# A fused layer of top-2 experts and gated delta-rule attention: expert rows gathered raw, weighed and scattered in token order, and added by accumulating transfers

## What is computed

```
xn  = (x - mean) / sqrt(var + 1e-5)
out = x + attention(xn) + ffn(xn)

ffn:       probs = softmax(xn @ Wg)          # 8 experts
           top-2 per token, their probabilities divided by their sum
           y_e = relu(xn @ W1[e] + b1[e]) @ W2[e] + b2[e]
           out = sum over the two experts of weight * y_e
attention: q, k, v = silu(conv4(xn @ Wq)), ...   # 8 heads, DK 128, DV 64
           gated delta rule over the 2048 tokens of a sequence
           (S = S * exp(g_t); u = (v_t - k_t S) * beta_t; S += k_t u; o_t = q_t S)
           out = (rmsnorm(o) * silu(xn @ Wg)) @ Wo
```

## Time and profile before

| | |
|---|---|
| median of 3 runs | 2579.6 us (2576.35 to 2581.1) |
| profiled execution, its own time | 2567.1 us |
| its span | 2565.4 us |
| PE busy | 2163.6 us (84%) |
| DVE busy | 1899.4 us (74%) |
| ACT busy | 1296.4 us (51%) |
| POOL busy | 1117.2 us (44%) |
| moved by DMA | 135.08 MB |
| routing, experts, attention | 0 to 253, 253 to 791, 791 to 2565 us |

### The profile page before, as it was taken

How to read it: one execution, slowest core, us unless ns; L and a number is a source line. 1 busy time by engine, 2 the same in 40 slices (tenths; PEclk the granted TensorE clock), 3 DMA queues, 4 the chain that set the end, 5 groups by cost and what they waited for, 6 DMA issues and landing times.

```text
span 2565.4 us, 89934 instructions
## 1 busy us (share of the span) xinstructions
PE 2163.6 (84%) x34781; PEld 1546.6 (60%) x34782; DVE 1899.4 (74%) x3928; ACT 1296.4 (51%) x3667; POOL 1117.2 (44%) x1123
## 2 busy tenths in 40 slices
PE   4441999999996798988989889898898988889886
PEld 4331889999883455555655646556565555655555
DVE  5544442232224998999989899999989999999896
ACT  0000344444333656656566565666656666566663
POOL 3555444444442262443724436254362533526333
PEclk9999999999998899999999999999999999999998
DMA  6564222222230100101010010100101001010000
GB/s 206 195 207 131 69 69 72 72 73 73 70 104 19 36 24 25 32 17 45 20 29 23 26 41 13 39 23 26 42 8 44 23 26 36 13 45 23 25 23 23
DMA packets 106769, 135.08 MB, mean 53 GB/s; under 512 B 39584, under 2 KB 80064, under 8 KB 106176
## 3 DMA queue, kind: packets, MB, share of 16 engines
q0 software_dynamic: 23296, 60.85, 7.6%
q1 hardware_dynamic: 65952, 48.91, 6.9%
q10 hardware_dynamic: 17184, 20.49, 2.3%
HBM read 76.18 MB, written 54.00 MB: 51 GB/s over the span
## 4 chain that ended last, share of the span: by engine, by line
PE 28%; DVE 26%; issue 8%; ACT 6%; DMA 1%; SPq 1%; DVEq 0%; ACTq 0%; PEldq 0%
PE att_psA L1078 9%; DVE att_cv L1540 8%; PE att_psC L1078 6%; DVE att_lane_t L1624 3%; DVE att_lanes L1626 3%; DVE att_S L1654 2%; PE att_psS L1092 2%; PE att_psC L1160 2%; PE att_psC L1183 2%; PE att_psS L1202 2%; PE att_psA L1120 2%; DVE att_O L1662 1%; DVE att_lanes L1612 1%; ACT att_t L1421 1%; ACT att_W L1434 1%
## 5 line engine op out<-in xcount | busy, mean ns | idle before, releaser
L1540 DVE SCALAR_TENSOR_TENSOR att_cv<-att_psA,att_cw,att_cv 128x508 f32<-128x508 f32 (+2 forms) x660 | 478.7, 736 | 7.6
L1078 PE MATMUL att_psA<-att_xt,att_wqkv 128*128 128x512 f32 x880 | 439.7, 633 | 14.2 <-DMA att_xt<-xn_cols 12.7
L1874 POOL TENSOR_TENSOR att_Sd<-att_S,att_mst 128x1024 f32<-128x1024 f32 x128 | 242.9, 1903 | 464.4 <-DVE att_S L1654 441.2
L804 PE MATMUL moe_psHT<-moe_xT,moe_w1s 128*128 128x128 f32 x2176 | 268.2, 277 | 0.3 <-issue 0.3
L1078 PEld LDWEIGHTS att_psA<-att_xt,att_wqkv 128*128 128x128 f32 x880 | 158.8, 196 | 179.1 <-issue 163.8
L814 PE MATMUL moe_psY<-moe_w,moe_hT 128*128 x1088 | 257.2, 379 | 0.0
L804 PEld LDWEIGHTS moe_psHT<-moe_xT,moe_w1s 128*128 128x128 f32 x2176 | 256.6, 194 | 0.9 <-issue 0.7
L669 ACT ACTIVATE moe_hT<-moe_psHT,moe_b1T 128x128 f32<-128x128 f32 x544 | 155.2, 368 | 201.0 <-PE moe_psHT L804 199.7
L768 DVE TENSOR_TENSOR moe_y<-moe_psY,moe_b2b 128x256 f32<-128x256 f32 x136 | 57.7, 424 | 255.0 <-PE moe_psY L814 154.5
L1540 DVE SCALAR_TENSOR_TENSOR att_cv<-att_psC,att_cw,att_cv 128x508 f32<-128x508 f32 (+2 forms) x300 | 213.9, 733 | 0.6
L814 PEld LDWEIGHTS moe_psY<-moe_w,moe_hT 128*128 128x128 f32 x1088 | 196.4, 190 | 21.1
(11 more groups left out here) (238 smaller groups left out, 4390.5 us busy)
## 6 DMA issues: line engine op xcount, KB each, us to landing
expert_out<-moe_y POOLq DMA_DIRECT2D x136, 128.0 KB
route_x_in<-in_L_attn_x_dram SPq DMA_DIRECT2D x64, 128.0 KB
moe_w<-in_L_ffn_W_dram SPq DMA_DIRECT2D x16, 512.0 KB
xn_rows<-route_xn ACTq DMA_DIRECT2D x16, 512.0 KB
xn_cols<-route_xnT ACTq DMA_DIRECT2D x16, 512.0 KB
att_xt<-xn_cols SPq DMA_DIRECT2D x16, 512.0 KB, 4.2
att_xr<-in_L_attn_x_dram SPq DMA_DIRECT2D x64, 128.0 KB, 2.8
out_dram<-att_xr SPq DMA_DIRECT2D x256, 32.0 KB
```

The lines of the kernel that those rows point to most:

```text
L804: last = nc.tensor.matmul(psHT[par][:, c * P:(c + 1) * P], w1s[:, par, d, c * P:(c + 1) * P], xT[:, par, d], start=(d == 0), stop=(d == DC ...
L1078: last = MM(pair_bank(m, j)[:, h, :], wqkv[:, c, (2 * j + h) * P:(2 * j + h + 1) * P], xt[:, c, :].rearrange("p (a l t) -> p l a t", a=GRO ...
L1540: last = V.scalar_tensor_tensor(out=late, in0=by_lane(pair_bank(m, j)[:, h, :])[:, :, 0:LT - d], scalar=cw[:, 2 * j + h, TAPS - 1 - d:TAPS ...
L1874: G.tensor_tensor(new, old, bc(mst[:, par, c, 4:4 + LANES, hs], 3, DV), op=ALU.mult).then_inc(s["sd_done" if two else "sd_half"], 1)
```

## The change

Each scattered row now carries a record of 8 words: SOURCE (the token), TARGET (its row in expert_rows), WEIGHT, MEAN and RSTD; 512 bytes are still written per row. xn_rows and its stores are gone. xnT has four buffers (COLS), and its copies wait for a store only from the fifth group on. The routing loops are written out for DVE, ACT and PE. DVE fills the record: mean and reciprocal deviation per group (L307, L321), the weights per iteration (L395 to L399), for which ACT does an Exp per iteration (L491). The tables slot and wtop, and the operations after the loop that made them, are gone; two spare regions with blank records are added.

```diff
+        COLS = 4
-        xnT = sb("xnT", [P, 2, DC, GT])
+        xnT = sb("xnT", [P, COLS, DC, GT])
...
+            pool.memset(record[:, :, :], 0.0).then_inc(cleared, 1)
...
+            for l in range(LANES):
+                r = slice(CT * l, CT * l + CT)
+                pool.wait_ge(consts, made + 1 + 2 * l)
+                pool.iota(fields[r, :, :, :, SOURCE], ...).then_inc(consts, 1)
+                pool.iota(fields[r, :, :, :, TARGET], ...).then_inc(consts, 1)
...
             dve.wait_ge(tr_done, g + 3)
-            dve.wait_ge(cols_stored[par], 16 * i + 16)
-            nc.vector.tensor_copy(xnT[:, par, 1], psT[:, par, 1]).then_inc(xnT_done, 1)
+            if g >= COLS:
+                dve.wait_ge(cols_stored[g % COLS], 16 * (g // COLS))
+            nc.vector.tensor_copy(xnT[:, g % COLS, 1], psT[:, par, 1]).then_inc(xnT_done, 1)
...
+            dve.wait_ge(second_done, i + 1)
+            V.tensor_scalar(total[:, :], second[:, :], 1.0, None, ALU.add).then_inc(weighed, 1)
+            dve.wait_ge(weighed, RECIPE * i + 1)
+            V.reciprocal(records[:, i, :, 0, WEIGHT], total[:, :]).then_inc(weighed, 1)
+            dve.wait_ge(weighed, RECIPE * i + 2)
+            V.tensor_tensor(records[:, i, :, 1, WEIGHT], records[:, i, :, 0, WEIGHT], second[:, :], op=ALU.mult).then_inc(noted, 1)
+            dve.wait_ge(noted, 5 * i + 5)
             V.tensor_copy(where[:, these, :], spot[:, these, :]).then_inc(located, 1)
...
-            with dve.Fori(2, NI) as i:
+            for i in range(2, NI):
...
-                act.dma_start(xn_v[g] ..., xn[:, par]).then_inc(rows_stored[par], 16)
...
+            def second_weight(i):
+                act.wait_ge(choose, CHOOSE * i + CHOOSE)
+                act.wait_ge(noted, 5 * i)
+                nc.scalar.activation(second[:, :], gap[:, :], ACT.Exp).then_inc(second_done, 1)
```

In the expert stage POOL gathers rows of x itself; DVE normalises them and keeps target and weight (L781, L783); after the second product it copies the target (L804), adds b2 (L805) and scales by the weight (L807), and POOL scatters the tile's rows into expert_rows, where the row of token n with its k-th expert is k * 8192 + n:

```diff
+            def normalise(q, par):
+                t = 2 * q + par
+                dve.wait_ge(x_loaded[par], 16 * q + 16)
+                dve.wait_ge(xtr, t + 1)
+                shift = ids.bitcast(F32)
+                nc.vector.tensor_scalar(xs[:, par], xt[:, par], shift[:, par, MEAN:MEAN + 1], shift[:, par, RSTD:RSTD + 1],
+                                        ALU.subtract, ALU.mult).then_inc(normed, 1)
+                nc.vector.tensor_copy(facts_of(t), ids[:, par, TARGET:WEIGHT + 1]).then_inc(normed, 1)
...
-                nc.vector.tensor_tensor(y[:, par], psY[par][:, 0:D], b2b[...], op=ALU.add).then_inc(y_done, 1)
+                dve.wait_ge(normed, 2 * t + 2)
+                nc.vector.tensor_copy(target[:, par, :], facts_of(t)).then_inc(y_step, 1)
+                nc.vector.tensor_tensor(y[:, par], psY[par][:, 0:D], b2b[...], op=ALU.add).then_inc(y_step, 1)
+                dve.wait_ge(y_step, 2 * t + 2)
+                nc.vector.tensor_scalar(y[:, par], y[:, par], target.bitcast(F32)[:, par, 1:2], None, ALU.mult).then_inc(y_done, 1)
...
-                pool.dma_start(yg_v[bass.ds(t, 1)]..., y[:, par]).then_inc(y_stored[par], 16)
+                pool.indirect_dma_start(yk_d[:, :], bass.IndirectOffsetOnAxis(ap=target[:, par, 0:1], axis=0), y[:, par], None).then_inc(y_stored[par], 16)
```

In the attention the gather and the two DVE operations per chunk are gone. POOL issues four accumulating DMAs at the end of chunk 1 and four at the end of chunk 2, which add the expert rows to xr while they land:

```diff
+            def add_rows(m, k):
+                if k == 0:
+                    G.wait_ge(xr_loaded, DONE * (m + 1))
+                else:
+                    G.wait_ge(y_added[0], DONE * (m + 1))
+                for l in range(LANES):
+                    G.dma_start(xr[lane_rows(l), :, :], y_v[k, l, bass.ds(m, 1)]..., accum_op=ALU.add).then_inc(y_added[k], 16)
...
             def out(m, c):
-                wait(dve, "acc2_done", n + 1)
+                if c in (0, 2):
+                    dve.wait_ge(y_added[1], DONE * (m + 1))
```

More of the change, by code:

```diff
@@ L162, in norm_and_route @@
         region = sb("region", [P, E]); region_i = sb("region_i", [P, E], I32)
[L163 to L166, removed]
+        record = sb("record", [P, NI, RECORDS + WIDE])
+        gap = sb("gap", [P, TI]); second = sb("second", [P, TI]); total = sb("total", [P, TI])
+        e8 = [sb(f"per_expert{i}", [P, E]) for i in range(4)]
         e8i = sb("per_expert_int", [P, E], I32)
@@ L217, in _ @@
                 sp.dma_start(tile[tuple(slice(None) for _ in tile.shape)], source).then_inc(loaded, 16)
+            sp.wait_ge(consts, NCONST)
+            for k in range(2):
+                row = E * (N + P) + k * P
+                sp.dma_start(ids_d[row:row + P, 0:RECORD], blank[:, E + k, :]).then_inc(rest_stored, 16)
             sp.wait_ge(rest_known, 1)
@@ L417, in link @@
                 dve.wait_ge(step, n[0])
-            weight, total, second, gap = r1
-            tot, tiles_f, end, base, zer8, tmp8 = e8
+            tot, tiles_f, end, zer8 = e8
             V.tensor_copy(rest[0:1, :], counted[0:1, :, 0]).then_inc(rest_known, 1)
-            link(V.tensor_tensor(gap[:, :], top2[:, :], top1[:, :], op=ALU.subtract))
-            gap_at = n[0]
             link(V.tensor_tensor(tot[:, :], taken, region[:, :], op=ALU.subtract))
@@ new lines, in second_weight @@
+            def second_weight(i):
+                act.wait_ge(choose, CHOOSE * i + CHOOSE)
+                act.wait_ge(noted, 5 * i)
+                nc.scalar.activation(second[:, :], gap[:, :], ACT.Exp).then_inc(second_done, 1)
+            deviation(0, 0)
+            columns(0, 0)
+            columns(1, 1)
+            for i in range(1, NI):
+                if i == 1:
+                    second_weight(0)
+                columns(2 * i, 0)
+                if i > 1:
+                    second_weight(i - 1)
+                columns(2 * i + 1, 1)
@@ L483, in _ @@
+            second_weight(NI - 1)
             for tile, source in attention_sources:
                 act.dma_start(tile, source).then_inc(attention_loaded, 16)
[L485 to L486 removed]
             nc.scalar.activation(expa[:, :], alog[:, :], ACT.Exp).then_inc(stats["expa_done"], 1)
[L488 to L491 removed]
+            for done in cols_stored:
+                act.wait_ge(done, 16 * (NG // COLS))
@@ L530, in _ @@
             columns_logits(1, 1)
-            with pe.Fori(2, NI) as i:
+            for i in range(2, NI):
                 columns_logits(i, 0)
@@ L596, in steps @@
                         between(sum(tile) + tile[0])
-            with eng.Fori(PEEL, MT // 2 - 1) as i:
+            with eng.Fori(PEEL, MT // 2 - 2) as i:
                 for tile in ((i, 1), (i + 1, 0)):
                     step(tile, after(*tile), before(*tile))
+            for tile in ((MT // 2 - 2, 1), (MT // 2 - 1, 0)):
+                step(tile, after(*tile), before(*tile))
             last = (MT // 2 - 1, 1)
@@ L834, with attention @@
 CREDIT = 4
-def attention(nc, keep, dims, loaded_params, NPARAM, xf, xnT_d, yg_d, stat_d, of):
+def attention(nc, keep, dims, loaded_params, NPARAM, xf, xnT_d, yk_d, stat_d, of):
     B, T, N, NT, NG, MT = dims
```

188 lines of the change are left out of this document (77 added, 111 removed).

## The result

The changed kernel takes 2612.1 us (median of 4, 2610.1 to 2614.1) against 2578.3 us on the same chip: 1.0136 times the time, interval 1.0121 to 1.0152, 34 us slower (the ratios here are of the runs beside each other; the two medians alone give 1.0131). The forecast was 2605, within 2541 to 2640, and slower; the direction and the range held, the sum of 26 us was 8 too small, and its parts were further off than the sum.

The account below looks back on a forecast made before the run. Experts bound by PE, attention mostly by a PE and DVE chain, routing by DVE's wait at L313 for late PE signals. 12 + 8 - 1 + 7 = +26 us on a median of 2579.6 gave 2605, range 2541 to 2640.

Parts of the forecast that it names:

- Routing, +12 forecast: Routing stage: 10 us for added DVE operations plus 2 us for the start, with the remote wait at L313 staying.
- the row stores: Routing: taking away 16 stores of 512 KB, on no path the rows show; zero, with a bound of a gain.
- the added operations: Routing: seven unhidden DVE additions per iteration, 1.4 us, over seven iterations: 10 us, bounds 4 and 16.
- the start: Start of routing: an added memset, nine iotas and a copy delay DVE's first work; +2 us (0 to 5).
- the first rival: Routing: the wait at L313 goes, POOL sets the stage, -51 us there, 2543 us in all; chance 0.25.
- PE's signal is held back: Routing: the 62.2 us wait at L313 is for PE's transposes, signalled late beside POOL's scatters, not for the column store.
- Experts, +8 forecast (3 to 28): Expert stage: loop stays PE's at 0, written-out tiles +6 us, first and last tile +2 us.
- the ring of POOL: Expert loop: y ready, scatter, gather, landing, normalising, W1's copy, scaling take 7.0 us against two tiles, 7.5; so no loss.
- The upper bound: Expert loop: at most 0.2 us for each of 108 tiles, 20 us, where the sum took 0.
- DVE's operations make the ring longer than 7.5 us: Expert stage, half of the rival "slower in the experts": 0.3 us a tile, 41 us, 2646 in all; chance 0.12.
- Attention, -1 and +7 forecast: Attention: 128 operations off DVE gain 1 us (0 to 61); the last group's wait for second additions costs 7 (2 to 9).
- halved: Routing rival: less traffic ahead of the scatters halves the wait at L313, -25 us, 2580 us in all; chance 0.1.

Follow-up runs that it names:

- e3: The change with two column buffers instead of four (COLS = 2), nothing else: 2613.7 us, ratio 1.0131 to the kernel before.
- e5: The kernel before, unchanged, traced a second time on another chip: 2529.0 us in the profiled execution.
- e12: The kernel before with four column buffers and the routing loops written out, row stores kept: 2559.0 us, ratio 0.9892 to the kernel before.
- e9: The change itself, unaltered, run again on the third chip: ratio 1.0111 to the kernel before.
- e6: The change without the accumulating transfers and their waits, so the experts' rows are left out of the output: 2564.6 us, ratio 1.0136 to the kernel before.
- e1: The change with DVE's copy of W1 put ahead of normalising the next gathered tile: 2601.3 us, ratio 1.0084 to the kernel before.
- e4: The change with the 16 row stores put back on ACT, and DVE's wait for them: 2623.5 us, ratio 1.0174 to the kernel before.
- e10: The change with W1's copy before normalising, gathers one tile further ahead, and the last group's adds one chunk earlier: 2618.5 us, ratio 1.0123 to the kernel before.

## Why the prediction was right, and where it was not

The direction was right, and so was the reading on which it stood, that the column buffers would not take the wait away. That the total came within 8 us is luck, since the routing and the experts erred by 15 and 26 us in opposite directions.

**Routing, +12 forecast, -3.5 found.** That the column buffers were not what DVE waited for was right: two and four give the same (e3), a chip without the wait exists (e5), and the wait moved to L380, which has no store among its conditions. That the wait would stay whole was wrong. DVE's remote waits fell from 62.2 to 48.5 us, and the kernel before, with four buffers and its loops written out, also ends the stage 12 us earlier (e12: 241.2). The step that failed is the term that is missing: the sum names the row stores, the added operations and the start, and nothing for the written-out loops, which stand only in the first rival. And "PE's signal is held back" was half of it: signals to PE, and DVE's to itself, are late as well. Set against e12 on the same chip, what the change adds costs 251.5 - 241.2 = 10 us (e9) where the sum had 12, but not as in the sum. The first scatter comes 4.8 us later (32.9 to 37.7), where I had 2 for the start; the rest, some 5 us, is what the added operations of DVE cost less what the missing row stores save, where I had 10 and 0. On the chip without waits, where POOL is the bound, the start is what is left: 205.3 to 209.0 (e6), 3.7 us.

**Experts, +8 forecast (3 to 28), +34 found.** This is the term that was wrong. The step that failed is the ring of POOL, 7.0 us against two tiles: it goes from W1's copy straight to the target, addition and scaling, and leaves out that PE's two products (2.02 and 1.89 us above) stand between them, since the first waits for that copy and DVE for the second. The real ring is 11.4 us for three tiles in the stretch shown and 11.8 by the loop's median, and it decides from 11.2 on, three tiles of 3.74. From first product to first product the 34 us are 24 in the loop, where the sum had 0 and e1 gives back 15; 8.3 in the 28 tiles written out, for the 6 forecast; and 0.9 and 1.0 at the head and behind the last product, for 2. What makes the loop's other 9 us, and whether it is DVE's work that makes the 8.3, no run shows. The upper bound, 0.2 us for each of the loop's 108 tiles, was near the loop's size; I had the right rival ("DVE's operations make the ring longer than 7.5 us") at 0.12. I had written in the text of the change that this wait stands ahead of the copy, and did not follow it to PE.

**Attention, -1 and +7 forecast, +5 found on one chip** (1783.8 to 1788.9), +12 between the first two traces. DVE's wait at the end is 8.6 us, of which 2.2 stood there before, so 6.3 for 7; the landing took 4.3 us in the median, not the 2.8 of the gather. Taking the 128 operations and the gather away gave 4 us (e5 to e6), not 1 and not 61; so small a difference is within what two traces of one program differ by.

**The sum.** -3.5 + 34.4 + 12 = 43 us between the two profiled executions, 34 between the medians; most of the rest is that the first trace of the kernel before lay 11 us under its median. Errors of -15, +26 and -1 us stand behind a total that was 8 us off.

**The rivals.** The wait's going (-51 us of stage) was no effect of the change, but it happened on another chip (-48 for the kernel before). It was not halved either: 62.2 to 48.5 us. The rule of the Trainium skill in "DMA: Bandwidth & Descriptors", Queues, rings and completion order, would have made the four buffers worth having, if the column stores' signals had stood behind scatters; by e3 they did not.

**Open:** what makes signals late on some chips while POOL issues indirect DMAs, and whether it belongs to the chip or to the occasion, since none was measured on two; why written-out loops shorten the stage; e4's 10 us; the experts' other 9 us; which part of e12's gain comes from the loops.

## What to carry to other kernels

When an instruction that waits for a transfer is put into an engine's queue, write down everything behind it on that engine and who waits for that, and close the ring to the transfer: count how many tiles it spans and divide. A busy share taken off an engine that stands in a latency chain can come back as waits (61 us off, 4 gained); to find it, compare the engine's waits, not its work. And a wait named "remote" can belong to the chip: take a second trace on another one before a change is built on it. And put a term into the sum for every part of a change, a rewritten loop too.

## What the runs showed of the hardware

Three things I had not expected. The kernel before took 2529 us on one chip and 2578 and 2587 on two others. Between the traces of the first two, the difference is in the routing stage (205.3 against 253.5 us), where DVE waited up to 12.5 us at a time for late signals on one chip and not at all on the other; in the change they are late to PE (27.8 us) as to DVE (48.5). The delay does not depend on how much the scatters write (46 us with 32 bytes per row, 49 with 512). And it is not bound to the routing: with gathers and scatters issued closer together (e10) DVE waited 58 us for "remote" in the expert stage, where the change itself, on a chip that shows the waits in its routing, has none.
